# Adding a unit's two output banks in one 128x1024 VectorE operation instead of two of 128x512

## The reference, cut to what matters

```python
def _L0_xattn_ref(x, latents, ...):          # x: 6404 context rows, latents: 1024 query rows
    q = rmsnorm(ln @ Wq) * scale             # 16 heads of 64
    k, v = rmsnorm(...), ...                 # keys: 6404 context rows and the 1024 rows themselves
    sim = jnp.einsum('bhid,bhjd->bhij', qn, kn)
    attn = jax.nn.softmax(sim, axis=-1)
    out = jnp.einsum('bhij,bhjd->bhid', attn, v)
    return out.transpose(0, 2, 1, 3).reshape(b, m, h * d) @ Wout + bout

def _L1_xattn_ref(x, context, ...):          # keys: one null key and the 6404 context rows
    ...
    attn = jax.nn.softmax(jnp.einsum('bhid,bhjd->bhij', q, k), axis=-1)
    out = jnp.einsum('bhij,bhjd->bhid', attn, v) @ Wo

x = x + tanh(g_xattn[0]) * L0_xattn(...);  x = x + tanh(g_ffn[0]) * L0_ffn(...)
x = x + tanh(g_xattn[1]) * L1_xattn(...);  x = x + tanh(g_ffn[1]) * L1_ffn(...)
```

## Time and profile before

| | us |
|---|---|
| median of 3 runs | 4764.76 (4763.67 to 4764.98) |
| the profiled execution's own time | 4763.29 |
| its span, first to last instruction | 4761.5 |
| TensorE busy in the span | 4319.0 (91%) |
| VectorE busy | 3613.2 (76%) |
| ScalarE busy | 3270.6 (69%) |
| mean granted TensorE clock | 0.946 of 2.4 GHz |

### The profile page before, as it was taken

How to read it: one execution, slowest core, us unless ns; L and a number is a source line. 1 busy time by engine, 2 the same in 40 slices (tenths; PEclk the granted TensorE clock), 3 DMA queues, 4 the chain that set the end, 5 groups by cost and what they waited for, 6 DMA issues and landing times. The chain is left out here.

```text
span 4761.5 us, 76929 instructions
## 1 busy us (share of the span) xinstructions
PE 4319.0 (91%) x25711; PEld 2658.2 (56%) x25711; DVE 3613.2 (76%) x5350; ACT 3270.6 (69%) x5554; POOL 506.0 (11%) x443
## 2 busy tenths in 40 slices
PE   2899979999699996999987699979998999979996
PEld 1566645666456664666655366646665566646654
DVE  6788868888688885888843588858886788768875
ACT  2899948999389993999922477737774677557770
POOL 2111111111111111111100100000000000000000
PEclk8899989999899997999988799989999999989997
DMA  2000000000000000000001000000000000000000
GB/s 51 1 0 0 0 3 1 0 0 0 3 0 0 0 0 1 0 0 0 0 36 47 3 0 0 1 2 0 0 0 2 0 0 0 2 0 0 0 0 9
DMA packets 15431, 19.45 MB, mean 4 GB/s; under 512 B 2704, under 2 KB 11256, under 8 KB 15096
## 3 DMA queue, kind: packets, MB, share of 16 engines
q1 hardware_dynamic: 9204, 14.52, 1.0%
q10 hardware_dynamic: 6148, 3.89, 0.3%
HBM read 17.87 MB, written 0.52 MB: 4 GB/s over the span
## 5 line engine op out<-in xcount | busy, mean ns | idle before, releaser
L647 DVE TENSOR_TENSOR a_probs_lo<-a_probs 128x1024 fp32r<-128x1024 f32 x1760 | 2112.3, 1222 | 580.4 <-ACT a_probs L562 322.0
L558 ACT ACTIVATE a_probs<-scores_ps,a_c_neg,a_k_rstd 128x512 f32<-128x512 f32 x1888 | 1315.1, 778 | 187.4 <-PE scores_ps L829 187.4
L562 ACT ACTIVATE a_probs<-scores_ps,a_c_neg 128x1024 f32<-128x1024 f32 x816 | 865.2, 1112 | 446.3 <-PE scores_ps L829 446.2
L854 PE MATMUL out_ps<-a_probs_lo,a_v 128*128 128x512 f32 x3520 | 1052.7, 420 | 0.0
L847 PE MATMUL out_ps<-a_probs,a_v 128*128 128x512 bf16 x3520 | 947.4, 388 | 12.0 <-DVE a_out_acc L660 12.0
L829 PE MATMUL scores_ps<-a_q_hi,a_k_hi 64*128 64x512 f32 x3520 | 795.1, 446 | 6.2 <-DVE a_k_lo L765 5.9
L854 PEld LDWEIGHTS out_ps<-a_probs_lo,a_v 128*128 128x128 f32 x3520 | 661.1, 188 | 186.6
L829 PE MATMUL scores_ps<-a_q_lo,a_k_hi 64*128 64x512 f32 x3520 | 706.6, 393 | 0.0
L829 PE MATMUL scores_ps<-a_q_hi,a_k_lo 64*128 64x512 f32 x3520 | 703.8, 393 | 0.0
L660 DVE TENSOR_TENSOR a_out_acc<-out_ps,a_out_acc 128x512 f32<-128x512 f32 x896 | 575.0, 683 | 58.9 <-PE out_ps L854 36.1
L847 PEld LDWEIGHTS out_ps<-a_probs,a_v 128*128 128x128 f16 x3520 | 302.6, 97 | 455.8 <-issue 202.5
(11 more groups left out here) (196 smaller groups left out, 3696.6 us busy)
## 6 DMA issues: line engine op xcount, KB each, us to landing
squares<-in_L_xattn_Wkv SPq DMA_DIRECT2D x16, 128.0 KB, 2.3
m_w<-in_L_ffn_w1T SPq DMA_DIRECT2D x1, 2048.0 KB, 7.7
m_w<-in_L_ffn_w2T SPq DMA_DIRECT2D x1, 2048.0 KB, 12.1
a_w_q<-in_L_xattn_Wq ACTq DMA_DIRECT2D x2, 512.0 KB
normed_T<-in_L_xattn_Wout SPq DMA_DIRECT2D x64, 0.5 KB
a_w_e<-in_L_xattn_Wo SPq DMA_DIRECT2D x64, 0.5 KB
residual<-in_x SPq DMA_DIRECT2D x1, 512.0 KB, 3.8
a_w_o<-in_L_xattn_Wout ACTq DMA_DIRECT2D x1, 512.0 KB
```

Of the source, the lines that this page charges most:

```text
L558: ins = nc.scalar.activation(probs[:, n % NB, e * 512:(e + 1) * 512], scores[:, n % 2, e * 512:(e + 1) * 512], ACT.Exp, bias=cneg[:, p:p + ...
L562: ins = nc.scalar.activation(probs[:, n % NB, :], scores[:, n % 2, :], ACT.Exp, bias=cneg[:, p:p + 1])
L647: nc.vector.tensor_tensor(plow[:, n % NPL, :], probs[:, n % NB, :], p_hi[:, n % NB], ALU.subtract).then_inc(plo_ready, 1)
L854: nc.tensor.matmul(outs[:, e * 512:(e + 1) * 512], v32[:, par, 2 * p + e, t, :], plow[:, n_ % NPL, e * 512:(e + 1) * 512], start=False, st ...
```

## The change

`add_out` no longer takes `e`. It waits once, until both banks are complete, and adds both with one operation of 128x1024: the source is `outs` seen as 2 x 512, the destination and second source are two rows of `oacc` at the same half of the queries, again 2 x 512, with a step of 1024 between the two rows. It raises `o_added` by 2 at once. The order on VectorE is unchanged, and nothing else in the program changes: TensorE still has both its waits on `o_added`.

```diff
-                def add_out(s, u, e):
+                def add_out(s, u):
 
                     p, n = u // 2, u % 2
-                    q = slice(n * 512, (n + 1) * 512)
-                    dve.wait_ge(mixed, 2 * s + e + 1 + MIX0)
-                    nc.vector.tensor_tensor(oacc[:, 2 * p + e, q], outs[:, e * 512:(e + 1) * 512], oacc[:, 2 * p + e, q],
-                                            ALU.add).then_inc(o_added, 1)
+                    acc = oacc[:, 2 * p:2 * p + 2, n * 512:(n + 1) * 512]
+                    dve.wait_ge(mixed, 2 * s + 2 + MIX0)
+                    nc.vector.tensor_tensor(acc, outs[:, :].rearrange("p (e q) -> p e q", e=2), acc, ALU.add).then_inc(o_added, 2)
...
-                                for e in range(2):
-                                    add_out(s0 + CT - 1, u, e)
+                                add_out(s0 + CT - 1, u)
...
                         if n % TAIL == 0:
-                            for e in range(2):
-                                add_out(g * NSTEP + NFULL * CT * GH + n - 1, n // TAIL - 1, e)
-                    for e in range(2):
-                        add_out((g + 1) * NSTEP - 1, GH - 1, e)
+                            add_out(g * NSTEP + NFULL * CT * GH + n - 1, n // TAIL - 1)
+                    add_out((g + 1) * NSTEP - 1, GH - 1)
```

## The result

The changed kernel takes 4771.67 us in the median of 20 launches (4768.68 to 4774.2), the kernel before 4764.76 us (4760.25 to 4769.23, 20 launches). The ratio is 1.0015 with a 95% interval of 1.0008 to 1.0022, so the change costs 7 us, between 4 and 10. The forecast was 4771.5 us, 6.7 more. The profiled execution of the changed kernel took 4770.06 us, its span is 4768.2.

A forecast was written before the change was run, and what follows sets the result against it. TensorE was taken to bound the kernel in both layers. Covered units 0, open tail borders 6.1 and null columns 0.6 gave +6.7 us, for a forecast median of 4771.5 us, range 4764.5 to 4777.5.

The forecast's parts named there:

- The bound: Full units in L0 and L1: TensorE sets the pace, 8.56 and 8.55 us a unit; VectorE's load has no say.
- The places: Loss only at 16 tail borders inside a pair of steps and 4 null-key places in L1; all else is covered.
- the null columns: Null key's columns in L1, line 765 behind the last full adds: 0.16 us later, 4 times, 0.6 us.
- The price of the operation: VectorE's merged 128x1024 add takes 1.22 us, between bounds of 1.21 and 1.36; two old adds take 1.28 to 1.29.
- VectorE's relief: VectorE over 448 units: 0.065 us saved in each, 29 us in all, none of it on the path.
- The delay at an open border: Tail borders inside a pair of steps: bank 1's high matmul comes 0.38 us later, 16 times, 6.1 us.
- Rival A: Open borders: the second high matmul still comes 0.60 us after the first, 5.9 us more, 4777.4 us; chance 0.08.
- B: Stepped 2 x 512 add is slow, deciding from 1.43 us on; at 1.6 us the time is 4793 us; chance 0.06.
- C: VectorE's relief counts in L0 after all: 14.6 us come off, giving 4756.9 us; chance 0.05.
- D: Tail delay is taken up by something late anyway, or the change does less; only 0.6 us stay, 4765.4 us; chance 0.07.

The follow-up runs named there:

- the two half versions: Against the kernel before (4762.92 us): wide add in full units only, 4762.34 us, ratio 1.0003; wide add in tails only, 4770.99 us, ratio 1.0016.
- the tails alone: One operation of 128x1024 in the tails, two adds in all full units, against the kernel before: 4770.99 us against 4762.92, ratio 1.0016.

## Why the prediction was right

*The bound* held: a period of 8.55 us in both layers, before and after, and the extra VectorE work behind the add, 283 us of it for some 5 us, confirmed it with a much larger dose than the change has.

*The places* held: 16 waits of the matmuls at the open borders, none elsewhere but at the null columns, and by time the two half versions give nothing and everything. Both causes were named beforehand: the add that waits for the second bank, and bank 0's matmul that can no longer start while bank 1 is being added.

*The price of the operation*, 1.22 us taken from line 698, was right to 2 ns. VectorE's relief was 26 us (29 forecast). The Trainium skill's formula ("VectorE: DVE Perf Modes", section "The TRN2 errata") gives 1224 ns for it, which agrees. The estimate of 71 us that follows from it for the saving does not, since two adds in a row overlapped.

*The delay at an open border* was mis-sized: 0.47 us and not 0.38. The step that failed is the start of the merged add, set at 0.226 us after the old one by the matmuls' spacing. It is 0.30, since the wide form starts 0.07 us later after the same signal than a narrow one; the spacing of the two high matmuls (0.24 instead of 0.227) makes up the rest. The same 0.07 makes the null columns 0.23 us late and not 0.16. By these sizes the sum is 8.4 and not 6.7 us. The measured 7, with an interval from 4 to 10, does not decide between the two sums; the traces do, with 0.47 a border and 8.2 us in the tails. The closeness of 4771.67 to 4771.5 is partly luck: a sum that was 1.7 us too small met parts outside the tails that were 1.5 us shorter in the profiled execution.

*Rival A*, a second high matmul that comes late, didn't happen: the two starts are 0.24 apart. *B* didn't: 1.222 us. *C* and *D* are refuted by the extra operation and by the tails alone.

*Two sentences on the profile were wrong.* The wait at an open border was to be about 1.3 us; it is 1.39. And the saved VectorE time was to show up as longer waits for ScalarE. The idle time before line 647, which waits for ScalarE, became shorter, from 580.4 us to 551.4, and it is the adds that now wait, 125.0 us for the low matmuls in 220 places, against 36.1 in 26. The merged wait holds VectorE 0.3 us in each unit of L1, and the `p_lo` behind it has so much less to wait for.

## What to carry to other kernels

When two operations on two buffers become one, look first at who waits for the first of them: a consumer that could start on buffer 0 while buffer 1 was in work now starts behind both, and the merged operation itself waits for both its inputs. The saving counts only where that engine sets the pace, the loss only where the signal has no cover, so count the places without cover, even if they are 16 of 448. And an engine idle at a dependency is a place for its own work: moving a score and a few matmuls into those gaps brought 9 us, where the adds' form had cost 7.

## What the runs showed of the hardware

A VectorE add of 128x1024 that waits for TensorE starts 0.07 us later after the matmul's signal than one of 128x512 (0.50 against 0.43 us after the last matmul's start). The step and the two banks are not the cause: two adds of 2 x 256 start at 0.43. Two adds of 128x512 in a row take 1.28 us and one of 128x1024 1.22.

An operation of POOL (GpSimd) got slower with VectorE at work next to it. Line 485, a power of 128x4, takes 1.01 us in the changed kernel and 1.94 in the run with the extra operation behind the add. The timelines of both at the same place, the changed kernel first:

```profile
606.70 1.01 POOL L485 TENSOR_TENSOR a_k_rstd<-a_k_stat,minus_half 128x4 f32<-128x4 f32 x1 [4.37 <-DVE a_k_stat L634]
606.99 2.57 DVE L647 TENSOR_TENSOR a_probs_lo<-a_probs 128x1024 fp32r<-128x1024 f32 x2 [0.37 <-ACT a_probs L558]
```

```profile
607.03 2.41 DVE L648 TENSOR_TENSOR a_probs_lo<-a_probs 128x1024 fp32r<-128x1024 f32 x2
607.18 1.94 POOL L486 TENSOR_TENSOR a_k_rstd<-a_k_stat,minus_half 128x4 f32<-128x4 f32 x1 [4.97 <-DVE a_k_stat L635]
```

In the first it starts while VectorE idles, in the second `p_lo` already runs. This holds throughout: the run with the extra operation behind the add has 244 of these POOL operations, and the 196 that start while a `p_lo` runs take 1.94 to 1.97 us, the other 48 take 1.00 to 1.23. In the changed kernel none starts inside a `p_lo`, and none takes over 1.23. It was off the path in both, but it would count where POOL is not.
